# An own order for the eight fill beats of a fused attention and feed-forward kernel

## The chip, the cores and the metric

The kernel runs on one core of one Trainium2 chip. The metric is the device time of the whole program in microseconds (us). A core has five engines that each work off their own instructions in order and wait for each other through semaphores: PE (TensorE, matrix products and transpositions), DVE (VectorE), ACT (ScalarE), POOL (GpSimd) and SP (SyncE, which here issues all transfers). PE writes to eight PSUM banks of 128 x 512 fp32.

## The reference

x has 4 batches of 512 tokens with 512 features. It is layer-normalised, goes through a causal attention with 16 heads of 32 (RMS-normed and rotated q and k) and, side by side, through a gated feed-forward with quantised weights of 1,408 hidden features:

```python
xn = _layernorm(x, axis=-1)
# attention of xn
q, k, v = jnp.split(jnp.einsum('bnh,hm->bnm', xn, w_qkv), 3, axis=-1)   # then 16 heads
q = rmsnorm(q, q_gamma); k = rmsnorm(k, k_gamma)
q = q * cos + rotate_half(q) * sin; k = k * cos + rotate_half(k) * sin
scores = jnp.where(mask, jnp.einsum('bhqd,bhkd->bhqk', q, k) / np.sqrt(HD), NEG)
s = jnp.einsum('bnh,hm->bnm', merged(softmax(scores) @ v), w_out)
# feed-forward of xn, W = (wq - 128) * scale
g = _silu(_qlinear(_silu(_qlinear(xn, gate)) * _qlinear(xn, up), down))
return x + s * g
```

## The kernel before

Every fp32 operand of a large product is split into a high part (rounded to the matrix engine's format) and a low part (the rest); a product is made of two or three partial products. ScalarE makes the high part by a copy, VectorE the low part by a subtraction. For weights that is `split_w(g)` (L596 on ScalarE, L793 on VectorE; g = 0 to 3 are four groups of four heads of `w_qkv`, g = 4 is `w_out`); for the transposed x it is `xt_high` and `xt_low`; for q and k it is `t_high` and `t_low`.

The work runs in beats: every engine has a function `beat(0, c)` that is called with c = -8 to 64, and which emits this engine's share of the beat in a fixed order. There are 64 attention units (4 batches x 4 groups x 4 token blocks or heads). In beat c:

- `project(c+7)`: q, k and v of one group of heads and one block of 128 tokens, 12 matmuls into the bank `QKV_PS` (L1055, L1073), in two halves
- `squares`, `inv_rms`, `unit_rms`, `rope`, `rope_sum` of unit c+6 (VectorE and GpSimd): the RMS norm and the rotation; `square(c+7)` on ScalarE reads the bank first (a square and a copy of v)
- `t_high`, `t_low`, `turn` (q, then k, both through the bank `W_PS`), `q_evac` and `k_evac` of unit c+5
- `maxima(c+4)`: products for the row maxima, through two banks `X_PS`
- `scores_t`, `exps`, `p_low`, `p_v` of unit c: the attention itself

The beats -8 to -1 are the fill: nothing of unit c exists yet. In them x of batch 0 is normalised (`ln_stats`, then `rstd_block` on GpSimd, then `ln_apply`), transposed by PE (`xn_turn`), and the weights are split. Into the beats are spread the gate and up products of the feed-forward, `gate_half(qq)`: 22 halves for each batch, 8 matmuls of 512 columns each, all through the one bank `GU_PS`. `FIRST` and `PER_BEAT` say in which beat they start and how many a beat has. `gu_weights` converts their integer weights on VectorE, `gated` and `gate` work up the result. After beat 64 come the remaining down products and the output.

What sets the order in the fill before the change, by engine:

- SP issues, in this order: x block 0, `w_qkv` group 0, the identity, x block 1, tables, gammas and mask, x block 2, group 1, x block 3, groups 2 and 3, `w_out`, the scales `s_gate`, `s_up`, and the rest.
- GpSimd, beat -8: `rstd_block(0, 0)`, then all 24 table products, then the wait for the two scales and `hsc` (L520, L522). `rstd_block(0, 1)` is in beat -7.
- ScalarE, beats -6 to -3: `t_high`, `xt_high`, gate, `split_w(c+7)`, then `q_evac`, `k_evac`, `square(c+7)`. `split_w(0)` stands ahead of all beats.
- VectorE (L941): `squares`, `t_low`, `v_low`, `gated`, `xt_low` and maxima, `unit_rms`, more maxima, `ln_stats`, `rope_sum`, `ln_apply`, `split_w` (beats of `SPLIT_AT`, L216), `gu_weights`.
- PE (L1204), beat c < 0: maxima, `xn_turn` of block c+7, gate half, `turn` of q, `project` first half, `turn` of k, `project` second half, second gate half. `project(n)` waits until all readers of unit n-1 are through with the one bank (`sq_ok`, `vh_ok`, `vl_ok`, `qn_ok` at n).

Of the kernel before, what the change touches and what calls it, by code (L numbers as in the profile page):

```python
# [18 lines left out]
P = 128  # L19
# [32 lines left out]
FIRST = (-3, -5, -5, -5)  # L52
PER_BEAT = ((2, 2, 2, 2, 2, 2, 2, 2, 2, 2, 1, 1),) + ((1, 2, 2, 2, 2, 2, 2, 2, 2, 1, 1, 1, 1, 1),) * 3
# [19 lines left out]
def build(nc, x, w_qkv, w_out, q_gamma, k_gamma, w_gu, s_gate, s_up, w_down, s_down,  # L73
          cos_tab, sin_tab, ident, mask_w, s_dram, rd_dram, wg_dram, hf_dram, out):
    top = ExitStack()
    with top:
# [139 lines left out]
        SPLIT_AT = (-8, -6, -5, -4, -3)  # L216
# [46 lines left out]
        def xt_bank(b, t):  # L263
            return GU_PS if b and t % 2 else W_PS

        def ln_at(r, c):


            if isinstance(r, int) and r == 0 and c < TB - 8:
                return 0, c + 8  # L270
# [21 lines left out]
        def _(sp):  # L292
# [17 lines left out]
            sp.dma_start(sgu[:, 0, :], s_gate).then_inc(sc_in, 16)  # L310
            sp.dma_start(sgu[:, 1, :], s_up).then_inc(sc_in, 16)
# [189 lines left out]
        def _(pool):  # L501
# [7 lines left out]
            def tables():  # L509

                pool.wait_ge(c_in, 16 * 5)
                for a in range(2):
                    for t in range(TB):
                        pool.tensor_tensor(cg[:, t, a, :], ctab[:, t, :], gam[:, a, :], ALU.mult).then_inc(tab_ok, 1)
                        for lo, hi in ((0, HD // 2), (HD // 2, 0)):
                            pool.tensor_tensor(sg[:, t, a, lo:lo + HD // 2], stab[:, t, lo:lo + HD // 2],
                                               gam[:, a, hi:hi + HD // 2], ALU.mult).then_inc(tab_ok, 1)
                pool.wait_ge(tab_ok, 2 * TB * 3)
# [15 lines left out]
            def rope(n, s, t):  # L534
                pool.wait_ge(qn_ok, n + 1)
                wait(pool, qp_ok, n)
                hh = HD // 2
# [29 lines left out]
            def beat(r, c):  # L567
                j, k = 16 * r + c, c % 4
                if there(j + 6, NB):
                    inv_rms(j + 6, (c + 6) % 2)  # L570
                if there(j, NB):
                    keep_past(j, 0)
# [7 lines left out]
                if isinstance(r, int) and r == 0 and c == -8:  # L580
                    tables()
# [13 lines left out]
        def _(act):  # L595
# [20 lines left out]
            def square(n, s, v, t):  # L616
# [3 lines left out]
                act.activation(sq[:, s, :, 0:HD], QKV_PS[:, 0:2 * GC].rearrange("p (h d) -> p h d", d=HD),  # L620
# [170 lines left out]
        def _(dve):  # L791
# [149 lines left out]
            def beat(r, c):  # L941
                j, k = 16 * r + c, c % 4
                attend, mxs, rms = there(j, NB), there(j + 4, NB), there(j + 6, NB)
                if rms:
                    squares(j + 6, (c + 6) % 2)
# [423 lines left out]
```

## Time and profile before

| | us |
|---|---|
| median of 3 runs | 742.36 |
| lowest and highest of them | 738.87, 744.09 |
| the profiled execution, its own time | 742.25 |
| span of its trace, first to last instruction | 740.1 |

Over the span PE is busy 667.6 us (90%), VectorE 557.5 (75%), ScalarE 448.3 (61%), GpSimd 397.6 (54%). These are averages; the first 70 us, to which the fill belongs, look otherwise. Times in the rows are us from the start of the span, and mean durations are ns where so marked. "Idle before" is time in which the engine stood still ahead of an instruction, with what released it.

### The profile page before, as it was taken

To read this page: it belongs to the slowest core of one execution; us is meant where nothing else is said; L and a number is where in the kernel's file an instruction comes from. 1 tells how busy PE (TensorE), PEld (TensorE's weight loads), DVE (VectorE), ACT (ScalarE), POOL (GpSimd) and SP (SyncE) were. 2 spreads that over 40 slices of the span, in tenths; PEclk is the share of its full clock that TensorE was granted. 3 is DMA by queue.
4 is the path that set the end of the run, shared out by engine and by line. 5 is a ranking of instruction groups with operands and counts; after the bars stand their busy time and mean duration, and the time that the engine had idled before them with its cause. 6 is when DMAs were issued, how large, how long until landed. Compare 5 with 4: busy or idle time off the path is not lost.

```text
span 740.1 us, 12539 instructions
## 1 busy us (share of the span) xinstructions
PE 667.6 (90%) x3648; PEld 559.3 (76%) x3648; DVE 557.5 (75%) x1387; ACT 448.3 (61%) x1007; POOL 397.6 (54%) x594
## 2 busy tenths in 40 slices
PE   2579999899999999999999999989999768759996
PEld 2568887778888888788888877878888646548885
DVE  2678888998788879988887899879776863555463
ACT  2445666687676667876766678757666844623331
POOL 5444556687565657775655678756565623310000
PEclk9999999999999999999999999999999867879999
DMA  8154443514434332144343321354633132558752
GB/s 308 38 182 147 158 157 101 172 58 131 115 101 115 101 101 74 33 127 122 94 122 95 101 73 48 79 161 124 180 116 120 65 104 62 150 191 296 266 213 100
DMA packets 57074, 94.39 MB, mean 128 GB/s; under 512 B 12336, under 2 KB 13104, under 8 KB 56880
## 3 DMA queue, kind: packets, MB, share of 16 engines
q1 hardware_dynamic: 57008, 93.59, 40.7%
q8 instruction: 31, 0.51, 0.3%
q14 instruction: 35, 0.29, 0.1%
HBM read 59.09 MB, written 25.82 MB: 115 GB/s over the span
## 4 chain that ended last, share of the span: by engine, by line
PE 64%; POOL 11%; DVE 8%; issue 7%; DMA 6%; ACT 2%; SPq 2%; DVEq 0%; POOLq 0%; ACTq 0%
PE bank L1176 17%; PE bank L1073 13%; PE bank L1199 10%; PE bank L1113 7%; PE bank L1152 6%; PE bank L1134 4%; POOL rr L532 4%; PE bank L1098 3%; PE bank L1085 3%; POOL pp L552 2%; DMA wd_raw<-w_down 2%; POOL rb L541 2%; POOL ra L538 2%; DVE pp L866 1%; POOL on L560 1%
## 5 line engine op out<-in xcount | busy, mean ns | idle before, releaser
L552 POOL TENSOR_SCALAR_AFFINE_SELECT pp<-pp 128x256 fp32r<-128x256 f32 x256 | 110.9, 445 | 159.2 <-DVE pp L866 158.9
L888 DVE CUSTOM_DVE_ANT_0 bank<-bank,msk_w 128x128 f32<-128x128 f32 (+3 forms) x256 | 121.1, 508 | 41.9 <-PE bank L1134 41.6
L866 DVE TENSOR_TENSOR pp<-pf,pp 128x512 fp32r<-128x512 f32 (+1 forms) x192 | 132.6, 690 | 17.2 <-ACT pp L657 17.2
L532 POOL TENSOR_TENSOR rr<-ss,half 128x8 f32<-128x8 f32 x64 | 109.4, 1709 | 55.2 <-DVE ss L834 55.2
L656 ACT ACTIVATE pf<-bank 128x512 f32<-128x512 f32 (+1 forms) x192 | 100.8, 525 | 43.0 <-PE bank L1098 36.7
L1073 PE MATMUL bank<-wq,xnt_h 128*128 128x384 f32 x512 | 115.1, 347 | 10.8 <-DVE qn L846 9.4
L1176 PE MATMUL bank<-xnt_h,wgu 128*128 128x512 f32 x352 | 99.2, 403 | 8.3 <-DVE g L916 4.6
L1113 PE MATMUL bank<-pp,va 128*65 128x512 f32 (+3 forms) x512 | 100.8, 316 | 5.7 <-POOL pp L552 4.4
L1073 PEld LDWEIGHTS bank<-wq,xnt_h 128*128 128x128 f32 x512 | 91.3, 194 | 15.0 <-issue 11.5
L657 ACT ACTIVATE pp<-bank 128x512 fp32r<-128x512 f32 (+1 forms) x192 | 101.2, 527 | 0.0
L1176 PE MATMUL bank<-xnt_l,wgu 128*128 128x512 f32 x352 | 96.4, 395 | 0.0
L1176 PEld LDWEIGHTS bank<-xnt_l,wgu 128*128 128x128 f32 x352 | 66.2, 188 | 16.3
L1113 PEld LDWEIGHTS bank<-pp,va 128*65 128x65 f32 x512 | 59.0, 139 | 23.2 <-POOL pp L552 7.9
L1176 PEld LDWEIGHTS bank<-xnt_h,wgu 128*128 128x128 f32 x352 | 60.4, 188 | 20.2 <-issue 10.4
L1199 PE MATMUL bank<-wd,ht_h 128*128 128x512 f32 x176 | 73.2, 416 | 2.6 <-DVE ht_l L938 2.6
L1199 PE MATMUL bank<-wd,ht_l 128*128 128x512 f32 x176 | 73.1, 415 | 0.0
L1134 PE MATMUL bank<-kst,qst 96*128 96x128 f32 (+3 forms) x256 | 71.1, 348 | 0.6 <-DVE mx L888 0.5
L1073 PE MATMUL bank<-wq,xnt_l 128*128 128x384 f32 x256 | 71.2, 361 | 0.0
L541 POOL TENSOR_TENSOR rb<-qn,sg 128x128 f32<-128x128 f32 x128 | 68.0, 552 | 0.0
L645 ACT ACTIVATE kst<-bank 96x512 fp32r<-96x512 f32 x64 | 38.1, 595 | 45.5 <-PE bank L1085 45.4
L1085 PEld LDWEIGHTS bank<-idr,tt 128*96 128x96 f32 x512 | 50.0, 127 | 18.8 <-DVE xnt_l L828 4.7
L1098 PE MATMUL bank<-qst,kst 97*128 97x512 f32 (+3 forms) x256 | 62.3, 321 | 0.7 <-ACT pp L657 0.7
(78 smaller groups left out, 1174.7 us busy)
## 6 DMA issues: line engine op xcount, KB each, us to landing
wgu<-wg_dram SPq DMA_DIRECT2D x66, 256.0 KB, 3.3
hf_dram<-g SPq DMA_DIRECT2D x44, 256.0 KB, 3.4
hf_raw<-hf_dram SPq DMA_DIRECT2D x44, 256.0 KB, 6.2
wg_dram<-wgu SPq DMA_DIRECT2D x22, 256.0 KB, 3.1
xr<-x SPq DMA_DIRECT2D x16, 256.0 KB, 4.8
stage<-w_gu SPq DMA_DIRECT2D x16, 256.0 KB, 3.5
oh<-oraw SPq DMA_DIRECT2D x64, 64.0 KB, 2.0
ol<-oraw SPq DMA_DIRECT2D x64, 64.0 KB, 2.0
```

The source lines that it names most:

```text
L532: pool.tensor_tensor(rr[:, s, :], ss[:, s, :], half[:], ALU.pow).then_inc(rr_ok, 1)
L552: op = pool.affine_select(pp[:, :, a:a + P], pp[:, :, a:a + P], [[0, 2], [1, P]], ALU.is_ge, 0.0, base=0, channel_multiplier=-1)
L656: act.activation(pf[:, tile], bank[:, 0:w], ACT.Exp, scale=SCALE)
L657: act.activation(ph[:, tile], bank[:, 0:w], ACT.Exp, scale=SCALE).then_inc(p_ok, 1)
L866: dve.tensor_tensor(pl[:, tile], pf[:, tile], ph[:, tile].bitcast(F32), ALU.subtract).then_inc(pl_ok, 1)
L888: op = dve.tensor_tensor_reduce(bank[:, a * w:(a + 1) * w], bank[:, a * w:(a + 1) * w], msk_w[:, N - w:N], 1.0, -3.0e38, ALU.add, ALU.max, ...
L1073: op = pe.matmul(QKV_PS[:, 0:3 * GC], x_[:, k, t * P:(t + 1) * P], wq[:, g, w_, k, :], start=(a == 0), stop=(a == len(todo) - 1))
L1098: op = pe.matmul(bank[:, c0:c0 + w], kst[0:KS + 1, par, h, j * P:(j + 1) * P], qst[0:KS + 1, par, h, j * P:N], start=True, stop=True)
L1113: op = pe.matmul(PV_PS[0:VW, j * P:N], va[:, v, j, h, :], part[:, a:a + w], start=(j == 0 and part is ph), stop=(j == 2 and part is pl))
L1134: op = pe.matmul(bank[:, a * w:(a + 1) * w], qst[0:KS, par, h, qb * P:(qb + 1) * P], kst[0:KS, par, h, 0:w], start=True, stop=True)
L1176: op = pe.matmul(GU_PS[:], wgu[:, s, k, :], x_[:, k, :], start=(a == 0), stop=(a == len(todo) - 1))
L1199: op = pe.matmul(DN_PS[t][:], h_[:, m, t * P:(t + 1) * P], wd[:, m, :], start=(m == 0 and h_ is ht_h[b % 2]), stop=(m == MT - 1 and h_ is ...
```

## The change

The diff, cut to its core:

```diff
-FIRST = (-3, -5, -5, -5)
-PER_BEAT = ((2, 2, 2, 2, 2, 2, 2, 2, 2, 2, 1, 1),) + ((1, 2, 2, 2, 2, 2, 2, 2, 2, 1, 1, 1, 1, 1),) * 3
+FIRST = (-4, -5, -5, -5)
+PER_BEAT = ((1, 1, 1, 1, 2, 2, 2, 2, 2, 2, 2, 2, 2),) + ((1, 2, 2, 2, 2, 2, 2, 2, 2, 1, 1, 1, 1, 1),) * 3
...
         def xt_bank(b, t):
-            return GU_PS if b and t % 2 else W_PS
+            return (GU_PS if t % 2 else W_PS) if b else (W_PS, GU_PS, X_PS[0], X_PS[1])[t]
+
+        def qkv_ps(n):
+            return PV_PS if n < 7 and n % 2 else QKV_PS
...
             load_x(sp, 0, 0)
-            load_w(0)
             sp.dma_start(idf[:], ident).then_inc(id_in, 16)
             load_x(sp, 0, 1)
+            load_w(0)
...
             load_x(sp, 0, 2)
+            load_x(sp, 0, 3)
             load_w(1)
-            load_x(sp, 0, 3)
+            sp.dma_start(sgu[:, 0, :], s_gate).then_inc(sc_in, 16)
+            sp.dma_start(sgu[:, 1, :], s_up).then_inc(sc_in, 16)
...
# GpSimd, beat
+                if c == -8:
+                    rstd_block(0, 0)
+                    rstd_block(0, 1)
+                    for t in range(TB):
+                        tables(t)
+                if c == -7:
+                    rstd_block(0, 2)
                 if there(j + 6, NB):
                     inv_rms(j + 6, (c + 6) % 2)
+                if c == -6:
+                    rstd_block(0, 3)
...
-                if isinstance(r, int) and r == 0 and c == -8:
-                    tables()
+                if c == -5:
+                    gate_scales()
...
# ScalarE, beat
-                if isinstance(r, int) and r == 0 and -6 <= c <= -3:
-                    split_w(c + 7)
                 o_out()
...
                 if there(j + 7, NB):
                     square(j + 7, (c + 7) % 2, (c + 7) // 4 % VR, (c + 7) % 4)
+                if -6 <= c <= -3:
+                    split_w(c + 7)
...
# VectorE, beats -8 to -1
+            def fill(c):
+                k = c % 4
+                if c == -8:
+                    ln_stats(0, 0)
+                    ln_stats(0, 1)
+                    dve.wait_ge(id_in, 16)
+                    dve.tensor_copy(idr[:], idf[:]).then_inc(idr_ok, 1)
+                    ln_apply(0, 0)
+                    split_w(0)
+                    return
+                for b, t in xt_at(c):
+                    xt_low(b, t)
+                if c >= -6:
+                    squares(c + 6, c % 2)
+                if c >= -5:
+                    t_low(c + 5, (c + 5) % 2)
+                if c >= -6:
+                    v_low(c + 6, (c + 6) // 4 % VR, (c + 6) % 4)
+                gated(half_at(c - 1, 1))
+                if c >= -4:
+                    maxima(0, c + 4, SM_A[k])
+                if c == -7:
+                    ln_apply(0, 1)
+                    ln_stats(0, 2)
+                if c == -6:
+                    ln_stats(0, 3)
+                    ln_apply(0, 2)
+                if c == -5:
+                    ln_apply(0, 3)
+                if c >= -6:
+                    unit_rms(c + 6, c % 2)
+                if c >= -4:
+                    maxima(0, c + 4, SM_T[k])
+                    maxima(0, c + 4, SM_B[k])
+                gated(half_at(c, 0))
+                if c >= -4:
+                    maxima(0, c + 4, SM_C[k])
+                if -6 <= c <= -3:
+                    split_w(c + 7)
+                if c >= -6:
+                    rope_sum(c + 6, c % 2)
+                gu_weights(half_at(c + 1, 0))
+                gu_weights(half_at(c + 1, 1))
...
# PE
-                else:
-                    wait(pe, xt_lo, n - 1 if b else n)
+                elif b:
+                    wait(pe, xt_lo, n - 1)
                     wait(pe, tk_ev, n_ + 1)
...
+                    free = n - 1 if n < 7 else n
+                    wait(pe, sq_ok, free)
+                    wait(pe, vh_ok, free)
+                    wait(pe, vl_ok, free)
+                    wait(pe, qn_ok, free)
...
-                    if part == 0 and early:
-                        for b, t in xts:
-                            xn_turn(j + 4, b, t)
...
                     if mxs:
+                        if c == -4:
+                            pe.wait_ge(xt_lo, TB)
                         maxima(r, c + 4, group[k])
...
                 if t_o is not None:
                     turn_k()
+                if c < TB - 8:
+                    xn_turn(0, 0, c + 8)
```

In words: the blocks of x of batch 0 get one PSUM bank each for their transposition, which PE now does at the end of beat t-8, behind the projection of unit t-1. Projections 1, 3 and 5 go to the bank `PV_PS`, so up to projection 6 PE waits for the readers of the unit before the last only. On VectorE the fill beats have their own function. Both halves of the weight splits change their place: on ScalarE from ahead of the evacuations to behind `square(c+7)`, on VectorE from behind `rope_sum(c+6)` to ahead of it. On GpSimd the wait for the scales moves from beat -8 to -5, and the reciprocal deviations ahead. Of the 22 gate and up halves of batch 0 four instead of six lie in the fill (one each from beat -4 on), and beats 7 and 8 have two each instead of one. `rope` of the first four units waits for the finished tables.

## Rows read from the trace of the kernel before

**Rows 1.** Windows: busy us (instructions) by engine, granted clock, DMA share, GB/s.

```profile
70.00:80.00 10.00, 10.00 (x57) 8.41 (x57) 8.30 (x24) 7.00 (x16) 6.38 (x10) 1.00 0.79 264
```

**Rows 2.** Chain that ended last, first 110 us: start us, us, what.

```profile
11.35 4.18 PE bank L1073 x12
...
31.39 2.26 PE bank L1073 x6
...
34.07 1.41 PE bank L1073 x6
...
55.55 1.05 PE bank L1073 x6
...
72.06 1.07 PE bank L1073 x6
...
74.59 1.86 PE bank L1176 x8
```

**Rows 3.** Timeline, fill and one later: start us, us, engine, line, operation [idle before, releaser].

```profile
5.87 1.48 ACT L599 ACTIVATE wq<-stage 128x1536 fp32r<-128x1536 f32 x1 [3.67 <-DMA stage<-w_qkv]
...
19.55 0.26 POOL L520 TENSOR_SCALAR hsc<-sgu 128x11 f32<-128x11 f32 x1 [4.76 <-DMA sgu<-s_up]
...
21.33 1.09 PE L1052 MATMUL bank<-idf,xr 128*128 128x128 f32 x4 [5.79 <-issue]
...
24.25 1.62 PE L1073 MATMUL bank<-wq,xnt_h 128*128 128x384 f32 x4 [1.83 <-DVE qn L846]
...
26.95 1.23 PE L1073 MATMUL bank<-wq,xnt_h 128*128 128x384 f32 x4
...
606.88 0.27 PE L1131 MATMUL bank<-idf,mx 128*4 128x128 f32 x1 [3.55 <-DVE mx L888]
```

**Rows 4.** Groups of instructions, 0 to 68.5 us: busy us, mean ns | idle before.

```profile
L796 DVE TENSOR_TENSOR wq<-stage,wq 128x1536 fp32r<-128x1536 f32 x4 | 7.0, 1752 | 0.0
...
L599 ACT ACTIVATE wq<-stage 128x1536 fp32r<-128x1536 f32 x4 | 5.9, 1486 | 3.7 <-DMA stage<-w_qkv 3.7
...
L834 DVE TENSOR_REDUCE ss<-sq 128x8 f32<-128x264 f32 x7 | 3.0, 424 | 0.8 <-ACT sq L620 0.6
L828 DVE TENSOR_TENSOR xnt_l<-bank,xnt_h 128x512 fp32r<-128x512 f32 x4 | 2.7, 686 | 1.6 <-ACT xnt_h L613 1.6
...
L620 ACT ACTIVATE sq<-bank 128x256 f32<-128x256 f32 x7 | 2.7, 381 | 11.2 <-PE bank L1073 11.2
...
L855 DVE TENSOR_TENSOR qp<-ra,rb 128x256 f32<-128x256 f32 x6 | 2.5, 424 | 3.3 <-POOL rb L541 3.3
L860 DVE TENSOR_TENSOR tt<-qp,tt 128x256 fp32r<-128x256 f32 x6 | 2.5, 422 | 1.4 <-ACT tt L633 1.4
...
L613 ACT ACTIVATE xnt_h<-bank 128x512 fp32r<-128x512 f32 x4 | 2.4, 597 | 8.9 <-PE bank L1052 8.9
...
L801 DVE TENSOR_TENSOR wo_l<-stage,wo_h 128x2048 fp32r<-128x2048 f32 x1 | 2.3, 2284 | 0.0
L927 DVE TENSOR_SCALAR wgu<-pf 128x512 fp32r<-128x512 int32 x6 | 2.3, 420 | 0.0
...
L911 DVE SCALAR_TENSOR_TENSOR g<-g,bank 128x512 f32<-128x512 f32 x3 | 2.0, 682 | 0.0
...
L602 ACT ACTIVATE wo_h<-stage 128x2048 fp32r<-128x2048 f32 x1 | 1.9, 1913 | 0.0
L623 ACT ACTIVATE va<-bank 128x128 fp32r<-128x128 f32 x7 | 1.9, 270 | 0.0
```

**Rows 5.** Windows of PE alone: length, busy, granted clock, DMA share, GB/s.

```profile
32.00:34.00 2.00, 2.00 (x11) 0.50 0.00 0
...
608.00:612.00 4.00, 2.80 (x8) 0.50 0.14 33
```

**Rows 6.** Windows of beats 7 and 8, from projection to projection, as rows 1.

```profile
137.49:146.94 9.45, 8.14 (x53) 6.73 (x51) 9.27 (x29) 6.82 (x17) 7.51 (x12) 1.00 0.31 98
146.94:153.90 6.96, 6.13 (x45) 5.57 (x45) 6.85 (x16) 5.57 (x15) 5.91 (x9) 1.00 0.31 98
```

More of the change, by code:

```diff
@@ L263, in xt_bank @@
         def xt_bank(b, t):
-            return GU_PS if b and t % 2 else W_PS
+            return (GU_PS if t % 2 else W_PS) if b else (W_PS, GU_PS, X_PS[0], X_PS[1])[t]
+        def qkv_ps(n):
+            return PV_PS if n < 7 and n % 2 else QKV_PS
         def ln_at(r, c):
-            if isinstance(r, int) and r == 0 and c < TB - 8:
-                return 0, c + 8
+            if c < 0:
+                return 0, None
             b, t = r + 1 + c // 16, c % 16 - 4
@@ L309, in _ @@
             sp.dma_start(stage[:, G * KT * 3 * GC:], w_out).then_inc(w_in[G], 16)
-            sp.dma_start(sgu[:, 0, :], s_gate).then_inc(sc_in, 16)
-            sp.dma_start(sgu[:, 1, :], s_up).then_inc(sc_in, 16)
             sp.dma_start(sdb[:], s_down.to_broadcast([P, H])).then_inc(sd_in, 16)
@@ L507, in _, with tables, gate_scales @@
             pool.wait_ge(ones_ok, 4)
-            def tables():
+            def tables(t):
                 pool.wait_ge(c_in, 16 * 5)
                 for a in range(2):
[L513 to L518, printed above, removed]
+                    pool.tensor_tensor(cg[:, t, a, :], ctab[:, t, :], gam[:, a, :], ALU.mult).then_inc(tab_ok, 1)
+                    for lo, hi in ((0, HD // 2), (HD // 2, 0)):
+                        pool.tensor_tensor(sg[:, t, a, lo:lo + HD // 2], stab[:, t, lo:lo + HD // 2],
+                                           gam[:, a, hi:hi + HD // 2], ALU.mult).then_inc(tab_ok, 1)
+            def gate_scales():
                 pool.wait_ge(sc_in, 32)
@@ L536, in rope @@
                 wait(pool, qp_ok, n)
+                if n < TB:
+                    pool.wait_ge(tab_ok, 6 * TB)
                 hh = HD // 2
@@ L839, in v_low @@
                 dve.tensor_tensor(va[:, v, t, :, HD:2 * HD],
-                                  QKV_PS[:, 2 * GC:3 * GC].rearrange("p (h d) -> p h d", d=HD),
+                                  qkv_ps(n)[:, 2 * GC:3 * GC].rearrange("p (h d) -> p h d", d=HD),
                                   va[:, v, t, :, 0:HD].bitcast(F32), ALU.subtract).then_inc(vl_ok, 1)
@@ L943, in beat @@
                 attend, mxs, rms = there(j, NB), there(j + 4, NB), there(j + 6, NB)
+                if c < 0:
+                    fill(c)
+                    return
                 if rms:
@@ L970, in beat @@
                     maxima(r, c + 4, SM_B[k])
-                if isinstance(r, int) and r == 0 and c == -8:
-                    dve.wait_ge(id_in, 16)
-                    dve.tensor_copy(idr[:], idf[:]).then_inc(idr_ok, 1)
                 if k == 0 and (c - 8) // 4 % 4 == G - 1 and there(4 * r + (c - 8) // 4, B * G):
@@ L993, in beat @@
                     ln_apply(b, t)
-                if isinstance(r, int) and r == 0 and c in SPLIT_AT:
-                    split_w(SPLIT_AT.index(c))
                 gu_weights(half_at(c + 1, 0))
@@ L1064, in project @@
                         pe.wait_ge(w_lo, g + 1)
-                    wait(pe, sq_ok, n)
-                    wait(pe, vh_ok, n)
-                    wait(pe, vl_ok, n)
-                    wait(pe, qn_ok, n)
+                    free = n - 1 if n < 7 else n
[3 more added lines that the diff above has]
+                    wait(pe, qn_ok, free)
                 todo = [(x_, a, k) for x_, a in ((xnt_h, 0), (xnt_l, 0), (xnt_h, 1)) for k in range(KT)]
```

9 lines of the change are left out of this document (4 added, 5 removed).

## The prediction

> **What bounds the kernel now.** I read the windows by stage first, then the chain that ended last, then the timeline of the fill, and last the groups of instructions for the price of each operation. The windows show two regimes. From about 70 us on the beats are bound by TensorE: in 70 to 80 us PE is busy 10.00 of 10 us [rows 1]. The eight fill beats (-8 to -1) are not. The chain shows what they are made of [rows 2]: projection 0 at 11.35 us for 4.18 us, projection 2 only at 31.39, projection 5 at 55.55, projection 7 at 72.06 us. I use the start of projection 7 as the fill's milestone, because from there the program is the same in both kernels, apart from two gate products. The hole between the first two is explained by the timeline [rows 3]: GpSimd stood 4.76 us before `hsc`, waiting for the load of `s_up`. The reciprocal deviation of the second x block was queued behind it, and so were the transposition and projection 1 (24.25 us). After that, a fill beat lasts 7 to 9 us. Its loop before the change is: the one projection bank must be read by VectorE's `unit_rms`, which waits for GpSimd's `rr`; meanwhile each weight split on ScalarE is issued early in the beat, and VectorE's half comes after `rope_sum`.
>
> **The start, step by step.** The load of `w_qkv` group 0 now goes behind `ident` and x block 1. Before, ScalarE could start its split at 5.87 us, released by that load [rows 3]. Ahead of it come 320 KB more (1,344 instead of 1,024 KB with its own bytes). At the mean rate that the rows allow (1,024 KB between the first issues and 5.87 us, so over 200 KB/us) this is 0 to 1.6 us; I take 1.0. Then: data 6.9, ScalarE split 1.49 and VectorE split 1.75 [rows 4] until 10.2, `xt_low` 0.69 until 10.9, projection 0 at 11.0 (0.35 earlier than now) with 4.18 us [rows 2] until 15.2. The transposition of block 1 stands behind it in PE's order: 1.1 as block 1's now at 21.33 [rows 3], until 16.3. `xt_high` 0.60 and `xt_low` 0.69 lead to projection 1 at 17.7 us instead of 24.25: 6.5 us gained, since the `s_up` wait is moved behind the statistics. Here two banks help too, as projection 1 needn't wait for `qn` 0. Its duration I take as now (24.25 to 28.18, 3.93 us [rows 3]), so it ends at 21.7.
>
> **What replaces the stall.** The decisive edit is a quiet one. On ScalarE `split_w(c+7)` moves from early in the beat to behind `square(c+7)`, so it waits for projection c+7. On VectorE `split_w(c+7)` moves from behind `rope_sum(c+6)` to ahead of it. VectorE waits for ScalarE's half; behind VectorE's wait stand `rope_sum`, and then the whole next beat: `xt_low`, `squares`, `t_low`. For `rope_sum` waits ScalarE's `t_high`, behind that stands `xt_high` of the next block, and for `t_low` waits PE's `turn_q`, which stands ahead of the next projection. So in beats -6 to -3 everything forms one ring: projection, square pair 0.65 (0.38 + 0.27), split on ScalarE 1.49, split on VectorE 1.75, `rope_sum` 0.42, `t_high` about 0.7 (two copies of the square's size, 0.38 and a little more, overlapped), `xt_high` 0.60, `xt_low` 0.69, `squares` 0.42, `t_low` 0.42 [rows 4], `turn_q` about 0.4, next projection.
>
> Step by step, ends of `rope_sum`, with some 0.05 us for each hop:
> - Beat -6: 21.7 + 0.65 + 1.49 + 1.75 + 0.42 = 26.05. That is about where it is now, so the 6.5 us are already spent.
> - Beat -5: 0.7 + 0.60 + 0.69 + 0.42 + 0.42 lead to `turn_q` at 29.05; 0.4, then projection 2 with its turn in the middle as now (31.39 to 35.48, 4.1 [rows 2]) until 33.6; 0.65 + 1.5 + 1.75 + 0.42: 38.05. The beat is 12.0 us.
> - Beat -4: 0.7 + 0.60 + 0.69 until `xt_low` of block 3 at 40.15, for which PE now waits ahead of the maxima; maxima 0.6; the gate product, 1.86 at full clock [rows 2], 2.9 after the long stop (below), until 43.7; turn 0.3; projection 3 with its turn 2.55 (72.06 to 74.59 [rows 2]) until 46.6; 4.3 through the splits and `rope_sum`, hops 0.2: 51.2.
> - Beat -3: the gate weights come last on VectorE, 0.4; gate product 2.9, turn 0.3, projection 4 2.6, square pair 0.65, then the split of `w_out`, 1.91 + 2.28, `rope_sum` 0.42 and hops: 63.0.
> - Beat -2, without a split: gate weights 0.4, gate product 2.9, turn and maxima 0.6: projection 5 at 67.1 instead of 55.55.
> - Beats -1 and 0: from projection 5 to 7 it is now 16.5 us with four gate products; with two of them (3.7 us) less it could be 12.8, but `squares`, GpSimd's `rr` and the maxima in VectorE's order don't shrink. I take 7.0 each: projection 7 at 81.1 instead of 72.06, **+9.1 us**.
>
> **The clock.** The granted clock fell to 0.50 (1.2 GHz) in 32 to 34 us, after a time in which PE was mostly stopped, and again in 608 to 612, after a stop of 3.55 us ahead of 606.88 [rows 3, 5]. Projection 1's first four matmuls take 1.62 us and its last four 1.23 [rows 3], where projection 7's first six take 1.07 [rows 2]: the same two levels. In the new fill PE stops 4 to 6 us in each of the beats -5 to -2. I charge each restart about 1 us (half speed over the first 2 to 3 us). The Trainium skill ("TensorE: Matmul & The Clock Gate", section "HAM oscillation") says that such gaps can put the engine back to the slow level in every round of a loop; that rule speaks against this change, and taken for the whole fill it is the third rival below.
>
> **The moved gate products.** The fill now holds four instead of six; beats 7 and 8 get a second one each. Each costs PE 1.86 and VectorE about 1.1 (a `gated` of 0.7 and the weights' 0.4). Beat 7 lasts 9.45 us with VectorE busy 9.27 and PE 8.14; beat 8 lasts 6.96 with 6.85 and 6.13 [rows 6]. By VectorE alone two of them cost 2.2 less 0.3 idle: 1.9. By PE alone with nothing hidden: 3.7. Between these, as both engines are nearly full, I take **+2.7**.
>
> **Costed at nothing.** x block 3 ahead of `w_qkv` group 1, and the two scale loads ahead of groups 2 and 3, delay the weights by at most 1 to 2 us; group 1 is needed at 22.4 us and now is there before 21; without that cover, up to 2 us. The wait for the finished tables in `rope` falls long after GpSimd's tables (now they end at 14.8, where the 4.76 us ahead of 19.55 begin [rows 3]). The first exponentials wait for the sixth gate weight, which now comes at the end of beat -1, just ahead of VectorE's beat 0; at most 0.5, contained in the 7.0. The loads of x for the next batch start a few us earlier, with nothing behind them in SP's order that is urgent. From beat 0 to 6 the engines' orders are unchanged, so the shift is carried to the end; PE fills that part, nothing gives it back.
>
> **Sum.** +9.1 + 2.7 = +11.8. The profiled execution took 742.25 us, 0.1 below the median of 742.36: 754.05, rounded **754 us**, 1.6% slower.
>
> **Rivals.**
> 1. *The same ring, PE at full clock* (13%). Then projection 1 takes 2.3 (-1.6), projection 2 2.6 (-1.5), three gate products 1.86 (-3.1): fill +2.9, sum +5.6, **748**. For it: projection 7 and the gate product behind it run at the full clock after fill beats in which PE has stops too [rows 2]. Against it: the new stops are longer.
> 2. *Faster: the splits lie under other work* (11%). This decides at one point: VectorE's split must be through when GpSimd's rope ends, so ScalarE's half must end about 2 us after `unit_rms` started. By my times for beat -6 it ends at 23.9, and rope at 22.0, less 1.75 needed: 3.6 us too late. If projections run further ahead than I think (second bank), the 6.5 us stay, the two gate products' 3.7 leave the fill, and beats 7 and 8 take back 2.7 to 3.7: about -7, **735**. The Trainium skill ("Perfetto Trace Analysis", section "Matmuls") advises exactly the second bank, so that reading one overlaps filling the next; by that rule the wait of each projection on `qn` goes. The chain agrees that `qn` lies on it now, but the order on VectorE decides here.
> 3. *PE slow all through the fill* (14%): projections 4.2 to 4.6, gate products 3.4, in beats -5 to -2: +9 more, **763**.
>
> **Numbers.** Forecast 62% for 754, own range 749 to 760. The range 747 to 763 leaves out the faster rival and the far side of the slow one, about 2 in 10. 1% is 7.4 us, about what a measurement of this kernel can tell from no change. Slower than 749.8: nearly all of the forecast (0.58) and rival 3, 0.72. Within 1%: rival 1, the forecast's low edge and a little of rival 2, 0.18. Faster: 0.10.
>
> **What would show it.** In the changed kernel: projection 1 near 17.7 us, projection 2 near 29.4, the starts of projections 2 and 3, and 3 and 4, 12 to 14 us apart; VectorE idle ahead of the splits of `wq`, released by ScalarE; ScalarE idle ahead of `t_high`; projection 7 near 81; beats 7 and 8 together near 19 instead of 16.4 us. It would be wrong if the fill's beats stay at 7 to 8 us, if VectorE's splits start without idle time, or if projection 7 comes before 72 us.

## The result and the profile after

The changed kernel takes 755.4 us (median of 4 runs, 754.85 to 755.84), the kernel before beside it 743.23 us (median of 4). The ratio is 1.0168 with a 95% interval of 1.0142 to 1.0194: slower by 1.7%. The forecast was 754. The span of the profiled execution is 753.0 us instead of 740.1.

To see where the 12.9 us arise, the start of the first half of each projection was read from both timelines of PE. Units are numbered as in the code; unit n is projected in beat n-7:

| unit | before | after | shift |
|---|---|---|---|
| 0 | 11.35 | 11.99 | +0.6 |
| 1 | 24.25 | 18.34 | -5.9 |
| 2 | 31.39 | 27.98 | -3.4 |
| 3 | 39.35 | 43.70 | +4.4 |
| 4 | 46.43 | 54.79 | +8.4 |
| 5 | 55.39 | 67.25 | +11.9 |
| 6 | 63.77 | 73.90 | +10.1 |
| 7 to 13 | 71.90 ... 126.97 | 80.88 ... 135.93 | +9.0, the same at all seven |
| 14 | 137.49 | 149.18 | +11.7 |
| 15 | 146.94 | 160.15 | +13.2 |
| 16 | 153.90 | 169.01 | +15.1 |
| 40 | 365.63 | 380.81 | +15.2 |
| 63 | 580.60 | 595.36 | +14.8 |
| end of the span | 740.1 | 753.0 | +12.9 |

(Here projection 7 starts at 71.90 in the timeline; the chain's row in [rows 2] has the same piece of work at 72.06.)

The chain of waits of the changed kernel, in order of time (start us, us, what), answers to [rows 2]. Its pieces named `issue`, for which the profile shows no releaser, are left out; here each is at most 0.14 us long:

```profile
11.99 4.19 PE bank L1133 x12
...
18.34 2.36 PE bank L1133 x12
20.73 0.38 ACT sq L636
21.11 0.17 ACT va L639
21.28 1.38 ACT wq L615
22.68 1.76 DVE wq L812
24.44 0.35 DVE qp L871
24.81 0.42 ACT tt L648
25.23 0.31 ACT tt L649
25.53 0.49 ACT xnt_h L629
26.05 0.69 DVE xnt_l L844
26.74 0.33 DVE ss L850
27.07 0.34 DVE tt L876
27.55 0.63 PE bank L1145 x4
28.18 2.03 PE bank L1133 x6
```

This is the ring of the prediction, link by link: projection 1, the square, ScalarE's half of the split, VectorE's half, `rope_sum`, `t_high`, `xt_high`, `xt_low`, `squares`, `t_low`, the turn of q, projection 2. No link stands elsewhere than was said. From the timeline of the changed kernel, the same places one beat on, with the idle time ahead in brackets:

```profile
34.66 1.76 DVE L812 TENSOR_TENSOR wq<-stage,wq 128x1536 fp32r<-128x1536 f32 x1 [5.28 <-ACT wq L615]
36.33 0.42 DVE L871 TENSOR_TENSOR qp<-ra,rb 128x256 f32<-128x256 f32 x1
...
36.78 0.42 ACT L648 ACTIVATE tt<-qp 128x256 fp32r<-128x256 f32 x1 [2.16 <-DVE qp L871]
...
38.92 1.09 PE L1194 MATMUL bank<-kst,qst 96*128 96x128 f32 x4 [5.42 <-issue]
...
39.81 2.02 PE L1236 MATMUL bank<-xnt_h,wgu 128*128 128x512 f32 x4
...
41.62 1.91 PE L1236 MATMUL bank<-xnt_l,wgu 128*128 128x512 f32 x4
```

VectorE stands 5.28 us for ScalarE's half, ScalarE then 2.16 us for `rope_sum`, PE 5.42 us for all of it. And behind its stop PE is slow: the eight matmuls of the gate product take 3.5 us from 39.81 on, against 1.86 in [rows 2]. The waits of VectorE, summed over the first 77 us, name the place without any reading of chains (engine, line, what it waited for: us in total, times, longest):

```profile
DVE wq L812 <- ACT wq L615: 12.4, 4, 5.3
DVE xnt_l L844 <- ACT xnt_h L629: 6.2, 3, 4.0
...
DVE wo_l L817 <- ACT wo_h L618: 3.3, 1, 3.3
```

Before the change no wait of VectorE for a weight's high part is among its longest, and in [rows 4] its splits have no idle time ahead. Together 15.7 us are new here. Of these 1.7 lie ahead of the first group's split at 9.53 us, behind its later load, and 14.0 in the ring. That is more than the shift of 9.0, since 5.9 us had been gained at projection 1.

The windows of beats 6 to 8, from projection to projection (length, then busy us and instructions of PE, its weight loads, VectorE, ScalarE, GpSimd; granted clock; DMA share; GB/s), the last two being those of [rows 6]:

```profile
135.93:149.18 13.25, 11.13 (x57) 9.01 (x55) 9.98 (x28) 6.76 (x15) 6.07 (x11) 0.88 0.65 209
149.18:160.15 10.97, 10.00 (x60) 8.28 (x59) 10.76 (x31) 6.51 (x17) 6.14 (x9) 0.99 0.45 135
160.15:169.01 8.86, 8.04 (x53) 6.92 (x53) 7.25 (x17) 6.41 (x16) 5.31 (x9) 1.00 0.45 131
```

Beat 7 now lasts 10.97 us instead of 9.45 and beat 8 lasts 8.86 instead of 6.96: +1.5 and +1.9. The first window, beat 6, is a surprise: 13.25 instead of 10.52 (126.97 to 137.49), 2.7 us, and the granted clock fell in it (0.88 on average).

### The profile page after: what moved, and what is told of

The parts are those of the page before. It is cut to its first block, busy times and chain, and to the rows that moved or that the text cites. A ratio compares the mean times of both kernels' runs of the same rounds, so it can differ in the third digit from the quotient of the medians.

```text
span 753.0 us, 12536 instructions
## 1 busy us (share of the span) xinstructions
PE 672.8 (89%) x3648; PEld 563.3 (75%) x3648; DVE 557.9 (74%) x1387; ACT 449.2 (60%) x1007; POOL 397.8 (53%) x594
## 4 chain that ended last, share of the span: by engine, by line
PE 67%; POOL 8%; DVE 8%; issue 6%; DMA 5%; ACT 3%; SPq 1%; DVEq 0%; POOLq 0%; ACTq 0%
PE bank L1236 19%; PE bank L1133 14%; PE bank L1259 9%; PE bank L1173 7%; PE bank L1212 6%; PE bank L1194 5%; PE bank L1158 4%; PE bank L1145 3%; POOL rr L537 3%; POOL pp L559 2%; DVE pp L882 2%; DVE bank L904 1%; POOL rb L548 1%; DMA wd_raw<-w_down 1%; POOL ra L545 1%
## 5 line engine op out<-in xcount | busy, mean ns | idle before, releaser
L672 ACT ACTIVATE pf<-bank 128x512 f32<-128x512 f32 (+1 forms) x192 | 100.9, 525 | 43.1 <-PE bank L1158 36.7
L1236 PE MATMUL bank<-xnt_h,wgu 128*128 128x512 f32 x352 | 102.1, 413 | 15.4 <-DVE wgu L943 9.5
L1133 PEld LDWEIGHTS bank<-wq,xnt_h 128*128 128x128 f32 x512 | 91.0, 193 | 14.8 <-issue 13.1
L1236 PE MATMUL bank<-xnt_l,wgu 128*128 128x512 f32 x352 | 99.3, 405 | 0.0
L1236 PEld LDWEIGHTS bank<-xnt_h,wgu 128*128 128x128 f32 x352 | 62.0, 193 | 27.4 <-DVE wgu L943 10.3
L1236 PEld LDWEIGHTS bank<-xnt_l,wgu 128*128 128x128 f32 x352 | 68.4, 194 | 17.0
```

The lines of the kernel that those rows point to most:

```text
L672: act.activation(pf[:, tile], bank[:, 0:w], ACT.Exp, scale=SCALE)
L1133: op = pe.matmul(qkv_ps(n)[:, 0:3 * GC], x_[:, k, t * P:(t + 1) * P], wq[:, g, w_, k, :], start=(a == 0), stop=(a == len(todo) - 1))
L1236: op = pe.matmul(GU_PS[:], wgu[:, s, k, :], x_[:, k, :], start=(a == 0), stop=(a == len(todo) - 1))
```

## Experiments

Each kernel was timed beside the kernel before. "Projection 7" is the start of unit 7; it is read from one profile, in which units 7 to 13 carry the same shift to some hundredths. All ratios are to the kernel before. One profile is one execution, and two things in the fill differ between executions of programs that are the same up to there. The start of projection 0 lies between 11.3 and 13.0 us in the kernels with the changed order of loads. And the stretches at the slow clock differ: projection 1 takes 2.4 us in the changed kernel and, after the same work and the same stop of 1.62 us, 3.7 us in the first experiment below. So a difference of 1 or 2 us at projection 7 is not yet the worth of an edit.

### One of the two split orders undone, and both

ScalarE's half back ahead of the evacuations:

```diff
+                if -6 <= c <= -3:
+                    split_w(c + 7)
                 o_out()
                 gate(half_at(c, 0))
...
                     square(j + 7, (c + 7) % 2, (c + 7) // 4 % VR, (c + 7) % 4)
-                if -6 <= c <= -3:
-                    split_w(c + 7)
```

> The changed kernel with one edit undone: ScalarE's half of the weight splits in beats -6 to -3 stands ahead of the evacuations again; VectorE's order stays as changed. My theory (the ring over the late splits): ScalarE's half is then done long before VectorE wants it, VectorE's splits start without idle time and lie under GpSimd's rope. Projection 7 starts near 63 us instead of 80.9 (before the change: 71.9), the time is about 737 us. Rival (the splits were hidden, the fill is slow for another reason, such as the slow clock or the four banks): projection 7 stays at 78 us or later, time 752 or more.

Measured: projection 7 at 65.50 us, 15.4 us earlier than in the changed kernel and 6.4 ahead of the kernel before. Time 741.45 us, ratio 0.9976 (0.9955 to 0.9997). The rival fell. The expectation was 2.5 us too low at projection 7, and 737 was too low for the time, as I had counted only part of the steps of beats 6 to 8: at unit 16 this kernel is 0.3 us behind the kernel before, so all of the 6.4 us are lost again on the way.

VectorE's half back behind `rope_sum`, ScalarE's left late:

```diff
-                if -6 <= c <= -3:
-                    split_w(c + 7)
                 if c >= -6:
                     rope_sum(c + 6, c % 2)
+                if -6 <= c <= -3:
+                    split_w(c + 7)
```

> The changed kernel with the other edit undone: on VectorE rope_sum stands ahead of split_w again; ScalarE's half stays behind the square of the same beat. My theory: VectorE still stops at the split until ScalarE has made its half, and the next beat's xt_low, squares and t_low stand behind it; only rope_sum and ScalarE's t_high leave the ring. Gain 1.1 to 1.7 us for each of two beats and about 0.4 for the other two: projection 7 near 77 us, time about 751 us. Rival (VectorE's order is the cause): as if both were undone, projection 7 near 65 us, 739 us.

Measured: projection 7 at 77.49 us, time 752.8 us, ratio 1.0127 (1.0094 to 1.016). Of the 15.4 us only 3.4 come back. The waits of VectorE in this kernel (first 75 us):

```profile
DVE wq L812 <- ACT wq L615: 9.1, 3, 3.5
...
DVE wo_l L817 <- ACT wo_h L618: 3.0, 1, 3.0
```

It stands 12.1 us instead of 15.7 (ahead of the first group's split 3.5 instead of 1.7, so in the ring 8.6 instead of 14.0). What makes the ring is that ScalarE's half was put behind the square, and so behind the projection of the same beat; VectorE's order only adds `rope_sum` and `t_high` to it.

Both back:

> The changed kernel with both halves of the splits in their old places. My theory: almost as with ScalarE's half alone undone, but about 1 us per beat slower, because VectorE's split no longer lies under GpSimd's rope: projection 7 near 66 us, time about 740 us. Rival: with both in place it is the fastest of the three, under 736 us.

Measured: projection 7 at 66.62 us, time 740.33 us, ratio 0.9955 (0.9936 to 0.9973). At projection 7 it is 1.1 us behind the version with ScalarE's half alone, 0.4 of which is there at projection 1. Whether it is faster or slower over all, the two intervals don't tell. Nor do the profiles: the one ran projection 1 at the slow clock (3.7 us instead of 2.3), the other the gate product of beat -2 (3.1 us instead of 2.1). What stands against a win from the split under the rope is told in the last section.

### The ring alone, in the kernel before

The two split orders of the change, and nothing else of it, put into the kernel before:

```diff
-                if isinstance(r, int) and r == 0 and -6 <= c <= -3:
-                    split_w(c + 7)
                 o_out()
...
                     square(j + 7, (c + 7) % 2, (c + 7) // 4 % VR, (c + 7) % 4)
+                if -6 <= c <= -3:
+                    split_w(c + 7)
...
+                if -6 <= c <= -3:
+                    split_w(c + 7)
                 if rms:
                     rope_sum(j + 6, (c + 6) % 2)
...
-                if isinstance(r, int) and r == 0 and c in SPLIT_AT:
-                    split_w(SPLIT_AT.index(c))
+                if c == -8:
+                    split_w(0)
```

> The kernel before with only the two split orders of the change: ScalarE's half behind the square of the same beat, VectorE's ahead of rope_sum. Theory: the ring arises without any other part of the change. The stall for the scales stays, so the loss of the ring comes on top: beats -6 to -3 last 10.5 to 13.5 us instead of 7 to 9, projection 7 starts near 85 us or later, time 755 to 760 us. Rival (the ring needs the other parts of the change): projection 7 within 3 us of 71.9.

Measured: 764.05 us, ratio 1.0302 (1.0272 to 1.0333), projection 7 at 93.36 us, more than the 755 to 760 us that were expected. The split orders suffice for the loss, and alone they cost 21.5 us: the starts of projections 1 to 5 are 25.36, 36.59, 49.78, 63.07 and 76.86, so 11 to 14 us apart. The rest of the change softened the loss.

### What the removed stall and the second bank are worth

The kernel before with the wait for the scales in beat -5:

```diff
                 pool.wait_ge(tab_ok, 2 * TB * 3)
+
+            def gate_scales():
                 pool.wait_ge(sc_in, 32)
...
                     tables()
+                if isinstance(r, int) and r == 0 and c == -5:
+                    gate_scales()
```

> The kernel before with one edit: GpSimd waits for the feed-forward's scales in beat -5 instead of beat -8; nothing else is moved. Theory: the stop of 4.8 us was worth its length and more. The reciprocal deviation of block 1 follows the tables at 14.7 us, projection 1 starts near 18 us instead of 24.25, the beats behind it keep their 7 to 9 us, projection 7 starts near 65.5 instead of 71.9, time about 736 us. Rival (something else is late next, such as the weights of group 1 or the integer loads): projection 7 at 70 us or later, time within 2 us of before.

Measured: 737.93 us, ratio 0.9946 (0.9924 to 0.9968). Projection 1 starts at 18.76 us (5.5 earlier), projection 7 at 67.17 (4.7 earlier). So the stall was worth most of its length, and one moved wait beats both kernels.

The same with two banks for projections 0 to 6 (`qkv_ps` and `free` as in the change):

> The kernel before with the later wait for the scales (alone 4.7 us at projection 7) and with two banks for the projections up to the sixth, nothing else. In the fill before, PE stood 3.3 us for unit_rms ahead of projections; if the second bank takes this away, projection 7 starts near 65 us and the time is about 735 us, ratio 0.990 to 0.993. Rival (the order on VectorE, in which t_low and the splits follow each other, sets the beat): projection 7 within 1 us of 67.2, time as with the scales alone.

Measured: projection 7 at 67.17 us, to the hundredth where it was with the scales alone; 737.52 us, ratio 0.9928 (0.99 to 0.9955). On the way it was ahead: projection 3 at 32.33 instead of 33.76, projection 4 at 40.04 instead of 41.70, projection 5 at 50.12 instead of 50.66. The gain is gone again by projection 6 (59.05 against 59.04). The rival's number came, but not for its reason. The timelines show what took the gain back, first with the scales alone:

```profile
48.22 1.17 PE L1180 MATMUL bank<-xnt_h,wgu 128*128 128x512 f32 x4 [1.80 <-DVE g L920]
49.23 1.10 PE L1180 MATMUL bank<-xnt_l,wgu 128*128 128x512 f32 x4
```

and with the second bank:

```profile
46.75 1.17 PE L1184 MATMUL bank<-xnt_h,wgu 128*128 128x512 f32 x4 [1.92 <-DVE g L923]
47.76 1.72 PE L1184 MATMUL bank<-xnt_l,wgu 128*128 128x512 f32 x4
```

The last gate product ahead of projection 5 starts 1.5 us earlier with the second bank. Then the granted clock is 0.50 from 48 to 51 us, where it is 1.00 without the bank, and from the start of that product to the fifth matmul of projection 5 it takes 4.65 us instead of 3.15: 1.5 us, just what had been gained. So in this order the bank won 1.5 us, and in this execution one fall of the clock took them back. Whether it falls there in every execution, one profile doesn't show, and the two intervals don't tell the times apart.

The changed kernel with ScalarE's half undone and one bank for all projections (`qkv_ps` returns `QKV_PS`, `free = n`):

> The changed kernel with ScalarE's half of the splits back in its old place and one bank for all projections, as before the change. It tells what the second bank is worth once the ring is gone. Expected: each projection waits for unit_rms of the unit before again, which costs 0.5 to 1.5 us in each of the beats -6 to -1, so projection 7 starts 3 to 8 us later than with two banks, time about 742 us. Rival (the chain over t_low and turn is as long anyway): within 1 us of the version with two banks.

Measured: 743.9 us, ratio 1.0021 (1.0001 to 1.0041), projection 7 at 69.60 us, 4.1 us later than with two banks. Of these up to 1.3 may be the start alone, as projection 0 begins at 12.77 us here and at 11.50 there, and with one bank everything behind waits for it; so the second bank is worth 2.8 to 4.1 us. Its worth hangs on the order around it: 1.5 us in the old order, which the clock took back, and 3 to 4 us in the new.

### The clock

Work added to the changed kernel behind `xn_turn` in four beats, to keep PE running where it stands:

```diff
+                for _ in range({-6: 30, -5: 24, -4: 18, -3: 24}.get(c, 0)):
+                    pe.matmul(ST_PS[0][:, 0:3 * GC], xnt_h[:, 0, 0:P], wq[:, 0, 0, 0, :],
+                              start=True, stop=True)
```

> The changed kernel with work added: behind beats -6, -5, -4 and -3 PE runs 30, 24, 18 and 24 more matmuls of 384 columns into a bank that nobody reads, in the time in which it otherwise stands. Nothing is left out. Theory (the restart at the slow clock costs 1 us or more per beat): the gate products of beats -4, -3 and -2 take 1.9 us instead of 3.5, 3.4 and 3.8, projection 2 is 1 to 1.5 us shorter, projection 7 starts 5 to 7.5 us earlier (near 74.5), time about 749 us. Rival (the durations at the slow level lie beside other work): projection 7 moves by under 2 us, time 754 or more.

Measured: 749.05 us, ratio 1.011 (1.0071 to 1.0148), projection 7 at 73.44 us. With 96 matmuls more the fill is 7.4 us shorter. From the timeline of this kernel, around the gate product of beat -4, which in the changed kernel took 3.5 us:

```profile
30.81 4.43 PE L1351 MATMUL bank<-wq,xnt_h 128*128 128x384 f32 x24
36.89 0.63 PE L1194 MATMUL bank<-kst,qst 96*128 96x128 f32 x4 [1.65 <-issue]
37.36 1.14 PE L1236 MATMUL bank<-xnt_h,wgu 128*128 128x512 f32 x4
38.34 1.09 PE L1236 MATMUL bank<-xnt_l,wgu 128*128 128x512 f32 x4
```

The 24 matmuls fill a stop of 5.4 us down to 1.65, and what comes behind runs at the full clock. So of the shift of 9.0 us at projection 7, 7.4 are the slow clock that the ring's stops bring with them, and with the ring at full clock the changed fill would be 1.5 us longer than the one before. Against the version without the ring, whose projection 7 starts at 65.50 us (with slow stretches of its own), the stops themselves cost 7.9 us and the clock 7.4. The Trainium skill ("TensorE: Matmul & The Clock Gate", section "HAM oscillation") describes this, a loop whose every round starts slow behind a wait; here the trace agrees, in four beats running (-5 to -2): in each the first work behind a stop of 4.2 to 6.4 us takes 1.7 to 1.8 times what it takes in the kernel with the filled stops.

### The moved gate products

The changed kernel with six gate products in the fill:

```diff
-PER_BEAT = ((1, 1, 1, 1, 2, 2, 2, 2, 2, 2, 2, 2, 2),)
+PER_BEAT = ((1, 1, 2, 2, 2, 2, 2, 2, 2, 2, 2, 1, 1),)
```

> The changed kernel with six gate products in the fill (one in beats -4 and -3, two in -2 and -1) and one each in beats 7 and 8, as before the change. My theory: the fill gets longer by 3 to 3.7 us (projection 7 near 84.5 us), and the three steps of the shift against the kernel before (2.7 us at unit 14, 1.5 at unit 15, 1.9 at unit 16; 6.1 in all) go away; time about 752.5 us. If the step of 2.7 us in beat 6 comes from the second integer load of that beat, it must be gone here too, though no gate product of beat 6 is touched. Rival (the steps have another cause): they stay, time 758 us.

Measured: 754.19 us, ratio 1.0152 (1.0109 to 1.0196). Projection 7 starts at 84.41 (+3.5), and the shift is 12.5 us at unit 7 and still 12.5 at unit 16. The time is 1.7 us over the expected 752.5, and of the 2.6 us won at unit 16 nothing is left at unit 63 (a shift of 15.2 against 14.8). All three steps are gone, the one of beat 6 too, although beat 6 has the same two products here as there. Its three windows now are as before the change:

```profile
139.48:150.01 10.53, 9.68 (x56) 8.04 (x55) 9.44 (x27) 6.40 (x15) 4.61 (x8) 1.00 0.72 237
150.01:159.45 9.44, 8.11 (x52) 6.71 (x51) 9.27 (x29) 6.84 (x17) 7.52 (x12) 1.00 0.34 98
159.45:166.44 6.99, 6.13 (x45) 5.57 (x45) 6.88 (x16) 5.60 (x15) 5.94 (x10) 1.00 0.30 97
```

So two gate products fewer in the fill gain 3.5 us there (2.9 of them from projection 5 to 7, where the products lie) and cost 6.1 us in beats 6 to 8. The times, 754.19 and 755.4, don't tell the two kernels apart. The step of 2.7 us in beat 6 is told by VectorE's timeline of the changed kernel: it waits for the integer weights of beat 7, now two loads instead of one, and PE's next gate product waits for what VectorE does behind that:

```profile
142.00 0.43 DVE L943 TENSOR_SCALAR wgu<-stage 128x512 fp32r<-128x512 int32 x1 [0.68 <-DMA stage<-w_gu]
143.24 0.43 DVE L943 TENSOR_SCALAR wgu<-stage 128x512 fp32r<-128x512 int32 x1 [0.81 <-DMA stage<-w_gu]
...
144.45 0.74 DVE L932 SCALAR_TENSOR_TENSOR g<-bank,hsc,g 128x512 f32<-128x512 f32 x1
...
145.33 1.49 PE L1236 MATMUL bank<-xnt_h,wgu 128*128 128x512 f32 x4 [2.12 <-DVE g L932]
146.62 1.91 PE L1236 MATMUL bank<-xnt_l,wgu 128*128 128x512 f32 x4
```

PE's stop is 2.12 us where it was 0.81 before the change, which makes 1.3 of the 2.7 us. The rest is the slow clock behind it: from 145.33 to the next projection it takes 3.85 us, before the change 2.42.

The loads are late because SP stood for the broadcast of the reciprocal denominators of beat 5, the first beat that has one (2.1 us, for the transfer that the broadcast reads); they are issued right behind it, at 136.04 and 137.03. Before the change they stood in the same place (126.53 and 127.86), but beat 6 needed only the first. The test moves them ahead of it:

```diff
-                first_batch(half_at(c, 0))
-                first_batch(half_at(c, 1))
+                if c != 6:
+                    first_batch(half_at(c, 0))
+                    first_batch(half_at(c, 1))
...
                 hidden_store(half_at(c, 0))
+                if c == 5:
+                    first_batch(half_at(6, 0))
+                    first_batch(half_at(6, 1))
                 if k == 1 and there((c - 5) // 4, B * G):
```

> The changed kernel with one thing moved on SP: the stores and integer loads of beat 6 are issued at the end of beat 5, ahead of the broadcast of the reciprocal denominators, for which SP otherwise stands. Theory (the step of 2.7 us in beat 6 comes from the second integer load landing late behind that wait): VectorE doesn't wait for integer weights in beat 6, the shift against the kernel before is unchanged at unit 13 (about 9.0 us) and under 10 us at unit 14 (now 11.7); steps at units 15 and 16 stay; time about 753 us. Rival (VectorE's second conversion or PE's second product in beat 7 makes the step): it stays at 2.7 us.

Measured: 752.77 us, ratio 1.015 (1.0115 to 1.0184). The shift is 9.0 at unit 13, 8.7 at unit 14, 10.1 at unit 15 and 12.0 at unit 16: the step of 2.7 is gone, the other two are as before. VectorE's conversions follow without a gap:

```profile
140.74 0.65 DVE L841 TENSOR_SCALAR xr<-xr,mv,rstd 128x512 f32<-128x512 f32 x1
141.31 0.75 DVE L947 TENSOR_SCALAR wgu<-stage 128x512 fp32r<-128x512 int32 x2
```

### What beats both kernels

ScalarE's half undone and six gate products in the fill:

> The changed kernel with ScalarE's half of the splits in its old place and six gate products in the fill (one each in beats 7 and 8). If the two effects add up: fill 3.5 us longer than with ScalarE's half alone undone, so projection 7 near 69 us, but no steps in beats 7 and 8 (6.1 us), so from unit 16 on 2.9 us ahead of the kernel before; time about 739.5 us, ratio about 0.996. Rival (the moved gate products find no room in a fill without stops): projection 7 at 71 us or later, ratio 1.0.

Measured: 737.26 us, ratio 0.9935 (0.9911 to 0.9959), projection 7 at 66.66 us. At projection 7 it is 1.2 us behind the version with four gate products, not 3.5; my sum of effects was too high by 2.3. The two products didn't get cheaper: from projection 5 to 7 it takes 16.5 us with them and 13.5 without, 3.0 more, and in the kernels with the ring 16.5 and 13.6. The difference arises in beat -4, where the two programs are the same. The version with four products ran its gate product there at the slow clock:

```profile
34.79 2.01 PE L1236 MATMUL bank<-xnt_h,wgu 128*128 128x512 f32 x4
36.60 1.81 PE L1236 MATMUL bank<-xnt_l,wgu 128*128 128x512 f32 x4
```

and this one at the full clock:

```profile
34.52 1.15 PE L1236 MATMUL bank<-xnt_h,wgu 128*128 128x512 f32 x4
35.51 1.10 PE L1236 MATMUL bank<-xnt_l,wgu 128*128 128x512 f32 x4
```

Its projection 3 starts 1.8 us earlier for that (36.69 against 38.51). Whether this is so in most executions is open. Steps in beats 7 and 8: none (shift -5.2 at unit 7, -4.8 at unit 16).

The same with VectorE's half still further ahead, before `unit_rms`:

```diff
                     maxima(0, c + 4, SM_A[k])
+                if -6 <= c <= -3:
+                    split_w(c + 7)
                 if c == -7:
                     ln_apply(0, 1)
...
-                if -6 <= c <= -3:
-                    split_w(c + 7)
                 if c >= -6:
                     rope_sum(c + 6, c % 2)
```

> As the version with ScalarE's half in its old place and six gate products in the fill, with VectorE's half moved further ahead, before unit_rms. With ScalarE's half undone, GpSimd's first rope product took 2.17 us instead of 0.73 while VectorE ran its 1.75 us split, as if GpSimd stood until the split was over. Theory (it stands for the access to memory, whatever it computes): the rope products are back at 0.73 and 0.87 us, and now GpSimd's rr (1.68) beside the split takes up to 1.4 us longer, little is won: projection 7 within 1 us of 66.7, ratio about 0.993. Rival (a small operation such as rr isn't held up): rr stays at 1.7, projection 7 starts 1 to 3 us earlier, ratio 0.990.

Measured: 738.33 us, ratio 0.9933 (0.9908 to 0.9958), but projection 7 at 71.07 us, 4.4 later than without the edit, which neither theory gave. 1.3 of it is there at projection 0 (12.97 against 11.64), where the two programs are the same; most of the rest arises between projections 4 and 5 (44.91 to 54.57 against 43.12 to 50.18), where the long split of `w_out` now stands ahead of `unit_rms` and `gated`. Of these 2.6 us, 0.9 are PE's longer stop ahead of the gate product (2.75 instead of 1.83) and 1.6 the slow clock in the product behind it (3.5 us instead of 2.0). The times don't show the 4.4 us: the two ratios are equal, and the profiled execution took 740.36 us, 2.0 more than the median. GpSimd's `rr` kept its duration, but it never began behind a split (last section).

## Why the prediction was right, and where it was not

**The mechanism.** Right, and shown: the edits of the split orders alone bring a loss into the kernel before, and undoing ScalarE's takes 15.4 us out of the changed one, far more than the 1 or 2 us by which executions differ. The forecast named both moved halves and did not weigh them; undone alone, ScalarE's is worth 15.4 us and VectorE's 3.4.

**The fill, +9.1.** Measured +9.0 at projection 7 (the forecast's own 81.1 less 72.06 is 9.04 as well). `rope_sum` ends at 24.8, 36.7, 50.6 and 62.4 us where the prediction had 26.05, 38.05, 51.2 and 63.0; projection 5 starts at 67.25 (67.1), projection 7 at 80.88 (81.1). Inside, errors cancel. The first weights came at 8.0 instead of 6.9 us, 2.1 later than before and beyond my bound of 1.6; this start varies, though: in the kernels that issue these loads in the same order projection 0 starts at 11.3 to 13.0 us. Projection 1 took 2.4 us, not 3.9, as it ran at the full clock; that it did so isn't settled by the program, since in one of nine kernels with the same work and the same stop ahead of it it ran slow. Projection 2 took 4.7 us, not 4.1. The gate products took 3.5, 3.4 and 3.8 us, not 2.9.

**The clock.** Undersized: I charged about 1 us for each restart; the run with the filled stops puts it at 7.4 us in all, where the difference between my forecast and rival 1 was 6.2, of which 1.6 were for projection 1, which wasn't slow. Its time, 749.05, is close to the 748 of that rival, but partly by luck: its fill is 1.5 us longer than before and not 2.9, and its steps in beats 6 to 8 are 6.6 us and not 2.7. Rival 3 (slow all through) was right for beat -5, where projection 2 ran at the slow clock to its end, and wrong for beats -4 to -2: there PE came back to the full clock with the end of the gate product or shortly behind it, and the projections took 2.6 to 3.1 us.

**The moved gate products, +2.7.** The term that was mis-sized: 6.1 us. The two steps in beats 7 and 8 are 1.5 and 1.9 (3.4 together, within my bounds of 1.9 and 3.7). The missing 2.7 is in beat 6, of which I had said that its orders are unchanged. They are, but the second product of beat 7 needs its integer weights converted in beat 6, and I had counted VectorE's 0.4 us for it and not its load, what that load stands behind on SP, and the slow clock behind PE's longer stop.

**"Nothing gives it back."** Wrong by 2.2 us: 15.1 at unit 16 became 12.9 at the end. 0.4 of it goes at unit 58 and the rest behind unit 63. From there the program is the same in all kernels, and it took 159.5 us before, 157.6 after, and 156.9 to 161.3 in the twelve experiments, one profile each, with no relation to what was changed. The stretch from unit 40 to 63 varies too, by -0.7 to +2.5 us against the kernel before. What sets these stretches in one execution is open, so the 2.2 us can't be put down to the change. The two errors of +3.4 and -2.2 nearly cancel: that 754 met 755.4 so closely is luck.

**The rivals.** The faster one named its point of decision as whether VectorE's split is done when GpSimd's rope ends. The point was off: with ScalarE's half in time the split lies under the rope in no beat (last section), and the kernel is faster all the same, since what counted was that nothing of the next beat waits for the projection of this one. The second bank, which the Trainium skill advises ("Perfetto Trace Analysis", section "Matmuls"), is worth 3 to 4 us in one order and 1.5 us in the other, where a fall of the clock took them back. The traces agree with the advice in both; what comes behind decides whether anything of it is left.

## What to carry to other kernels

When the two halves of a job on two engines move in their orders, ask of each what it now stands behind: a long half placed behind a consumer of this round's product ties all rounds into one ring, and no freed buffer helps. Price a moved piece of work with everything that it needs one step earlier, its loads above all, and look at what those stand behind in their queue. And where a change makes a matrix engine stop for some us in every round, add what the slower clock costs behind each stop; here that was 7.4 us, about as much as the stops themselves. A gain of 1 or 2 us can go the same way, so compare the level of the clock before you put a small difference down to an edit.

## What the hardware did that I had not expected

**GpSimd stands while VectorE splits.** In the version with ScalarE's half undone, VectorE's split starts just before GpSimd's first rope product:

```profile
28.49 1.75 DVE L812 TENSOR_TENSOR wq<-stage,wq 128x1536 fp32r<-128x1536 f32 x1
...
28.66 2.18 POOL L545 TENSOR_TENSOR ra<-qn,cg 128x256 f32<-128x256 f32 x1 [0.54 <-DVE qn L862]
30.80 0.86 POOL L548 TENSOR_TENSOR rb<-qn,sg 128x128 f32<-128x128 f32 x2
```

`ra` takes 2.18 us there, and 0.73 in the changed kernel (20.72 and 29.46 us), where VectorE does nothing long beside it. GpSimd's product ends 0.6 us after the split, as if most of it had run only then. So the two took turns in beats -6 and -5, and in beats -4 and -3 the split began only at the end of the rope or behind it (39.92 against 38.39 us, and 46.52 against 46.54). The Trainium skill ("Advanced Engine Details and Errata", section "Mode Summary") says that VectorE's second port is shared with GpSimd, so that GpSimd's instructions and VectorE's two-port ones block each other. This trace shows such a block, for a subtraction of two fp32 tensors; whether that is a two-port instruction in the section's sense, no run here shows. The other order looks different. In the last version GpSimd's `rr`, a power over 8 values per partition, had begun 0.26 us before the same split, and both kept their durations:

```profile
19.11 1.66 POOL L537 TENSOR_TENSOR rr<-ss,half 128x8 f32<-128x8 f32 x1 [1.03 <-DVE ss L850]
...
19.37 1.76 DVE L812 TENSOR_TENSOR wq<-stage,wq 128x1536 fp32r<-128x1536 f32 x1
```

It is so in each of the three beats in which they meet (`rr` begins 0.26, 0.37 and 1.44 us ahead). So no run shows whether `rr` would be held up behind a split, and the question of that experiment stays open.

**The granted clock in the windows starts at 1.00.** In both kernels the first projection's matmuls take 1.62 us for four, as at 1.2 GHz (projection 1 of the changed kernel: 0.93), while the windows of that stretch show 1.00; in the kernel before the windows show 1.00 up to 31 us and 0.50 only behind that [rows 5], although projection 1 took 1.62 us for four at 24.25 us too. At the start of these traces the durations, not the clock column, tell the level.
